# Large tiles moved to multiples of 2048 bytes, and the first block's probabilities transposed on TensorE

## What is computed

```python
x = x + tanh(g_xattn) * attention(layernorm(x), ctx, ctx)   # causal, softmax, concat @ Wo.T + bo
x = x + tanh(g_ffn) * ffn(layernorm(x))
# ffn: h = silu((x @ w1.T) * s1) * ((x @ w2.T) * s2)         256 -> 1024
#      h = gelu((h @ h1.T) * hs1); h = gelu((h @ h2.T) * hs2) 1024 -> 1024, twice
#      return (h @ w3.T) * s3                                1024 -> 256
```

## Time and profile before

| | |
|---|---|
| median of three runs | 1804.46 us (1802.91 to 1806.54) |
| the profiled execution | 1806.88 us, of which the span from the first to the last instruction is 1804.8 us |
| TensorE busy | 1730.7 us, 96% |
| VectorE, ScalarE, GpSimd busy | 1321.6, 1306.7, 1106.8 us |
| mean granted TensorE clock | 0.985 of full |
| first FFN matmul | 89.43 us after the start |
| span per block after it | 1715.4 us over 31 blocks of FFN beside attention and one alone |

### The profile page before, as it was taken

One profiled execution on the slowest core, in us unless ns is written; L12 is line 12 of the kernel. 1 busy time (PEld: TensorE's weight loads), 2 busy tenths in 40 slices (PEclk: granted clock), 3 DMA queues, 4 the chain that ended last, 5 costly groups with the idle time before them and its releaser, 6 DMA issues.

```text
span 1804.8 us, 39555 instructions
## 1 busy us (share of the span) xinstructions
PE 1730.7 (96%) x11014; PEld 1465.8 (81%) x11014; DVE 1321.6 (73%) x2803; ACT 1306.7 (72%) x3014; POOL 1106.8 (61%) x1646
## 2 busy tenths in 40 slices
PE   3399999999999999999999999999999999999998
PEld 2288888888888888888888888888888888888876
DVE  5767777777777777777777777777778777777764
ACT  3477777777777777777778777778777777777764
POOL 4666566567556567656567656656655656755652
PEclk8699999999999999999999999999999999999999
DMA  9944545544455544445554454554445554445420
GB/s 288 242 108 109 131 128 142 141 111 116 122 134 134 139 121 113 120 128 134 139 129 114 114 131 128 145 136 113 114 129 132 137 139 114 114 121 134 117 59 7
DMA packets 370970, 231.37 MB, mean 128 GB/s; under 512 B 283136, under 2 KB 340736, under 8 KB 369408
## 3 DMA queue, kind: packets, MB, share of 16 engines
q1 hardware_dynamic: 368784, 219.23, 47.7%
q10 hardware_dynamic: 2160, 11.81, 1.9%
HBM read 113.53 MB, written 41.94 MB: 86 GB/s over the span
## 4 chain that ended last, share of the span: by engine, by line
PE 91%; issue 2%; DMA 2%; POOL 2%; ACT 1%; DVE 1%; SPq 1%; POOLq 0%; DVEq 0%; ACTq 0%
PE ffn L976 71%; PE work L916 12%; PE s_bank L951 3%; PE pv L967 3%; PE work L1056 2%; DMA pT<-p_parts 1%; POOL p_parts L468 1%; POOL p_parts L466 1%; DMA aw<-in_attn_w 0%; DMA q<-q_saved 0%; POOL hb L513 0%; ACT probs L821 0%; SPq L360 0%; SPq L356 0%; POOL ha L508 0%
## 5 line engine op out<-in xcount | busy, mean ns | idle before, releaser
L976 PE MATMUL ffn<-hb,W 128*128 128x512 f32 x2048 | 512.2, 402 | 1.4 <-POOL hb L513 1.4
L976 PE MATMUL ffn<-ha,W 128*128 128x512 f32 x2048 | 492.1, 397 | 0.8 <-POOL ha L508 0.8
L658 DVE TENSOR_REDUCE full<-ffn 128x256 f32<-128x512 f32 x512 | 349.5, 688 | 194.1 <-PE ffn L976 194.1
L976 PEld LDWEIGHTS ffn<-ha,W 128*128 128x128 f32 x2048 | 379.4, 188 | 90.6 <-POOL ha L508 1.7
L976 PEld LDWEIGHTS ffn<-hb,W 128*128 128x128 f32 x2048 | 377.6, 188 | 86.3 <-POOL hb L513 2.3
L821 ACT ACTIVATE probs<-probs,exp_bias 128x128 f32<-128x128 f32 x1024 | 320.4, 390 | 50.8 <-POOL exp_bias L476 49.7
L468 POOL TENSOR_TENSOR p_parts<-probs,p_parts 128x512 f16<-128x512 f32 x256 | 300.4, 1173 | 20.5
L513 POOL TENSOR_TENSOR hb<-full,hb 128x256 fp32r<-128x256 f32 x256 | 187.3, 737 | 122.3 <-ACT full L839 116.5
L976 PE MATMUL ffn<-x2T_hi,W 128*128 128x256 f32 x1024 | 258.5, 287 | 1.4 <-DVE x2T_lo L754 0.9
L839 ACT ACTIVATE full<-full,cols 128x256 f32<-128x256 f32 x512 | 253.1, 494 | 0.0
L976 PE MATMUL ffn<-x2T_lo,W 128*128 128x256 f32 x1024 | 252.9, 284 | 0.0
(11 more groups left out here) (82 smaller groups left out, 2341.1 us busy)
## 6 DMA issues: line engine op xcount, KB each, us to landing
k<-k_saved SPq DMA_DIRECT2D x256, 128.0 KB, 2.8
q<-q_saved SPq DMA_DIRECT2D x256, 128.0 KB, 2.8
k_saved<-k_parts SPq DMA_DIRECT2D x32, 512.0 KB, 3.2
q_saved<-q_parts SPq DMA_DIRECT2D x32, 512.0 KB, 3.1
wnat<-in_ffn_w ACTq DMA_DIRECT2D x11, 1024.0 KB, 7.5
xT<-in_x_T SPq DMA_DIRECT2D x32, 256.0 KB, 3.3
cT<-in_ctx_T SPq DMA_DIRECT2D x32, 256.0 KB, 3.4
x_in<-in_x SPq DMA_DIRECT2D x32, 256.0 KB, 3.7
```

Source lines behind the costliest of these rows:

```text
L658: dve.tensor_reduce(full[:, m % 4], src[:].rearrange("p (a t) -> p t a", a=2), AX_X, ALU.add).then_inc(done, 1)
L976: return pe.matmul(dst, w, h, **flags)
```

## The change

1. The small tiles are declared first, then a tile of 264 floats that nothing reads or writes (`to_boundary`), then W, aw and all large tiles. With the scratch region cut from 8192 to 4096 bytes, W starts at 14336, a multiple of 2048 bytes, and so does every tile behind it whose predecessors are whole multiples of 2048 bytes, which all large tiles are.
2. In block 0 the eight D steps go. In their place TensorE transposes the 8 x 128 columns of p_parts into a bank of the FFN (step T, 16-bit), and ScalarE copies the bank to pT (step R). R stands in for the landing of the transfer: it raises pT_in by 16. T.k waits for the split, and for R.(k-2), whose bank it overwrites; R.k waits for T.k and PV.(k-2).
3. PROLOGUE is a new order of the same steps, with T and R for D. ORDER is unchanged; the blocks from 1 on keep their DMA transposes.
4. GpSimd makes a 16-bit copy of the identity matrix before it clears k4, and VectorE and TensorE wait for one more of GpSimd's constants before they start.

```diff
 PROLOGUE = steps("""
-    q.0 kw Q.0 K qw q.1 k st W.0 kr.0 v Q.1 V W.1 S.0 S.1 e.0 S.2 W.2 s.0 m.0 S.3 Q.0+ qr.0 K+ s.1 i.0 m.1 s.2 e.1
-    S.4 kr.1 m.2 i.1 S.5 s.3 lx+ m.3 i.2 lr W.3 lc+ q.0+ W.4 s.4 m.4 p.0 e.2 S.6 S.7 s.5 e.3 W.5 p.1 s.6 lt+ qr.1
-    i.3 D.0 D.1 m.5 Q.1+ D.2 p.2 nh.0 i.4 k+ PV.0 PV.1 PV.2 p.3 i.5 nm.0 D.3 e.4 qw+ W.6 p.4 PV.3 p.5 PV.4 i.6 kw+
-    s.7 st+ W.7 PV.5 To.0 O.0 e.5 D.4 q.1+ m.6 V+ m.7 S.0+ W.8 nm.1 i.7 D.5 PV.6 W.9 p.6 nh.1 W.10 p.7 F.0 rx PV.7
-    S.1+ qr.0+ To.1 O.1 e.6 nm.2 nh.2 e.7 o.0 s.0+ kr.0+ n2.0 F.1 D.6 nm.3 nh.3 to.0 v+ to.1 m.0+ X2.0 i.0+ s.1+ o.1
-    n2.1 e.0+ D.7 kr.1+ x2.0 rx+ qr.1+ lr+ x2.1 m.1+ X2.1
+    Q.0 k q.0 q.1 W.0 st i.0 W.1 v K Q.1 e.0 i.1 V W.2 S.0 kw qw e.1 S.1 W.3 kr.0 i.2 S.2 S.3 Q.0+ s.0 m.0 p.0 qr.0
+    lr p.1 s.1 m.1 R.0 T.0 rx s.2 K+ m.2 W.4 s.3 p.2 q.0+ S.4 W.5 i.3 i.4 e.2 W.6 PV.0 R.1 T.1 s.4 m.3 S.5 qr.1 m.4
+    p.3 s.5 lc+ i.5 W.7 kr.1 m.5 s.6 i.6 Q.1+ p.4 PV.1 p.5 S.6 i.7 nm.0 m.6 nh.0 T.2 nm.1 S.7 T.3 lt+ p.6 s.7 PV.2
+    e.3 R.2 lx+ PV.3 T.4 k+ qw+ T.5 PV.4 qr.0+ p.7 PV.5 T.6 e.4 e.5 R.3 m.7 To.0 q.1+ nh.1 O.0 e.6 st+ R.4 W.8 R.5
+    nh.2 V+ W.9 W.10 to.0 PV.6 T.7 F.0 e.7 o.0 S.0+ PV.7 To.1 R.6 F.1 nh.3 kw+ R.7 nm.2 s.0+ kr.0+ n2.0 O.1 nm.3
+    X2.0 X2.1 v+ m.0+ to.1 i.0+ o.1 x2.0 kr.1+ n2.1 rx+ S.1+ lr+ x2.1 s.1+ e.0+ qr.1+ m.1+
 """)
...
-        W = sb("W", [P, W_COLS], F32R)
-        aw = sb("aw", [P, 4, KE, E])
-        wq, wk, wv, woT = (aw[:, i] for i in range(4))
+        COPIES = 4
+        PSLOTS = 4
+        TSLOTS = 2
+
...
+        ident16 = sb("ident16", [P, P], F16)
...
+        wait_holder = sb("wait_holder", [P, 1])
+
+        to_boundary = sb("to_boundary", [P, TO_BOUNDARY])
+
+        W = sb("W", [P, W_COLS], F32R)
+        aw = sb("aw", [P, 4, KE, E])
+        wq, wk, wv, woT = (aw[:, i] for i in range(4))
+        x_in = sb("x_in", [P, ROWS, E])
         xres = sb("xres", [P, ROWS, E])
...
+        pT_turned = sem("pT_turned")
...
-                    if kind == "D" and here:
+                    if kind == "D" and here and not (isinstance(blk, int) and blk == 0):
...
+            pool.wait_ge(pool_const, 6)
+            pool.tensor_copy(ident16[:], ident[:]).then_inc(pool_const, 1)
             pool.memset(k4[:].bitcast(F32), 0.0).then_inc(keys_cleared, 1)
...
-                    pool.wait_ge(pool_const, 9)
+                    pool.wait_ge(pool_const, 10)
...
+                    if kind == "R" and weights:
+                        act.wait_ge(pT_turned, k + 1)
+                        wait(act, pv_ready, k + 1 - TSLOTS)
+                        act.activation(pT[:, k % TSLOTS].rearrange("p a h s -> p (a h s)"),
+                                       ffn[1 + k % 2][:].bitcast(F16), ACT.Copy).then_inc(pT_in[k % 2], 16)
...
+                        if kind == "T" and weights:
+                            pe.wait_ge(p_hi_ready, k + 1)
+                            pe.wait_ge(p_lo_ready, k + 1)
+                            pe.wait_ge(wq_centred, 1)
+                            if k > 1:
+                                pe.wait_ge(pT_in[k % 2], 16 * (k // 2))
+                            turned = ffn[1 + k % 2][:].bitcast(F16)
+                            for i in range(8):
+                                last = pe.transpose(turned[:, i * P:(i + 1) * P], p_parts[:, k % 2, i // 4, i % 4],
+                                                    ident16[:])
+                            last.then_inc(pT_turned, 1)
...
-    nc = bacc.Bacc("TRN2", target_bir_lowering=False, num_devices=1, dynamic_dma_scratch_size=8192)
+    nc = bacc.Bacc("TRN2", target_bir_lowering=False, num_devices=1, dynamic_dma_scratch_size=4096)
```

More of the change, by code:

```diff
@@ L23 @@
 LOW_BITS = 0xFFF
+TO_BOUNDARY = 264
 MASKED = -1e9
@@ L121, in program @@
         flag = sb("flag", [1, 1], I32)
-        x_in = sb("x_in", [P, ROWS, E])
         stats = sb("stats", [P, ROWS, 6])
@@ L128, in program @@
         rstd = sb("rstd", [P, ROWS])
+        vs = sb("vs", [P, ROWS, H, VCOLS], BF16)
+        negmax = sb("negmax", [P, PSLOTS, 4])
+        exp_bias = sb("exp_bias", [P, PSLOTS, 4])
+        head_sum = sb("head_sum", [P, 2, PAIR, D])
+        rden = sb("rden", [P, ROWS, H])
+        stats2 = sb("stats2", [P, ROWS, 6])
+        moments2 = sb("moments2", [P, ROWS, 2])
+        var_eps2 = sb("var_eps2", [P, ROWS])
+        rstd2 = sb("rstd2", [P, ROWS])
+        wait_holder = sb("wait_holder", [P, 1])
[4 more added lines that the diff above has]
+        x_in = sb("x_in", [P, ROWS, E])
         xres = sb("xres", [P, ROWS, E])
@@ L131, in program @@
         cT = sb("cT", [P, KE, TOK])
-        COPIES = 4
         q_parts = sb("q_parts", [P, 2, ROWS, KE, P], F32R)
@@ L139, in program @@
         k_saved = nc.dram_tensor("k_saved", [2, ROWS, P, KE * P], F32, kind="Internal").ap()
-        vs = sb("vs", [P, ROWS, H, VCOLS], BF16)
         v_rest = sb("v_rest", [P, ROWS, E])
-        PSLOTS = 4
         probs = sb("probs", [P, PSLOTS, 4, P])
-        negmax = sb("negmax", [P, PSLOTS, 4])
-        exp_bias = sb("exp_bias", [P, PSLOTS, 4])
         p_parts = sb("p_parts", [P, 2, 2, 4, P], F16)
-        TSLOTS = 2
         pT = sb("pT", [P, TSLOTS, 2, 4, P], F16)
-        head_sum = sb("head_sum", [P, 2, PAIR, D])
-        rden = sb("rden", [P, ROWS, H])
         heads = sb("heads", [P, ROWS, E])
@@ L154, in program @@
         x1_prev = sb("x1_prev", [P, ROWS, E])
[L155 to L158, removed]
         x2n = sb("x2n", [P, ROWS, E])
-        wait_holder = sb("wait_holder", [P, 1])
         x2T_hi = sb("x2T_hi", [P, KE, TOK], F32R)
@@ L548, in _ @@
         def _(dve):
-            dve.wait_ge(pool_const, 9)
+            dve.wait_ge(pool_const, 10)
             def scale_constants():
@@ L1079, in _ @@
             any_inexact = []
-            pe.wait_ge(pool_const, 9)
+            pe.wait_ge(pool_const, 10)
             run(False, 0)
```

## The result

The changed kernel takes 1782.03 us, the median of four runs (1781.86 to 1783.53), where the kernel before took 1805.5 us beside it (1802.91 to 1808.18): ratio 0.9871, 95% interval 0.9855 to 0.9886. The forecast was 1800.5 us, in a range from 1793 to 1806.5. The sign was right. The size was wrong by a factor of six: 23.5 us came where 3.9 were forecast.

A forecast was written before the change was run, and what follows sets the result against it. TensorE, busy 96% of the span, bounds the kernel; only prologue length and matmul pace can move it. Start and middle 1.5 us plus tail 2.4 make 3.9 us off the 1804.46 us median: 1800.5 us, range 1793 to 1806.5.

The forecast's parts named there:

- Aligned tiles: Large tiles moved to multiples of 2048 bytes: priced at nothing for the matmuls, with the extreme outcomes left to two rivals.
- rival 3: All blocks: tile starts set the matmul pace; 125 us less, 1676 us, or a part of it; chance 0.11.
- Rival 4: All blocks: aligned tiles slow matmuls as two operands on one boundary; 0.002 us each, 15 us, 1816 us; chance 0.03.
- The prologue: Stretch before the first FFN matmul: 3.9 us shorter, that matmul at about 85.5 us instead of 89.4.
- T: Block 0, eight TensorE transposes per step: 0.9 us, lower end 0.39, upper end twice 0.86; covered except for the last.
- R: Block 0, ScalarE copy of 1024 elements out of PSUM: 1.1 us, between 0.6 and 1.89; eight make 8.8 us.
- First scores: Start of the prologue: K's copy first, Q's parts about 1.3 us earlier, scores at 30.8 us instead of 31.98.
- The middle: ScalarE's queue from first to eighth exponentials: 36.35 us of work, 3.0 of waits, ending 72.75 instead of 74.25 us.
- The tail: From the end of the eighth exponentials to the first FFN matmul, 15.2 us before: 2.4 us less.
- Rival 1: Prologue hardly shorter: ScalarE keeps its old 6.3 us of chunk waits; 0.6 us left, about 1804; chance 0.18.
- Rival 2: Prologue slower: R in ScalarE's queue holds the chunk chain, from R of 1.7 us on; about 1807; chance 0.08.
- The clock: TensorE's half speed in the first FFN matmuls: 1.7 us either way; gained only if transposes count as activity.

The follow-up runs named there:

- the fourteen profiles: Profiled kernels that all have the new prologue and differ only in where their tiles lie: first FFN matmul between 81.9 and 85.9 us, 84.0 on average.
- e11: Changed kernel with the old tiles and DMA transposes instead of T and R, two block 1 loads moved ahead: 1832.97 us, ratio 1.0149.
- e2: Changed kernel with the tiles where they were before (new order, T and R kept): 1800.74 us, ratio 0.9965.
- e10: Kernel before, old order and old tiles, with T and R in place of the DMA transposes in block 0: 1819.94 us, ratio 1.0071.
- e3: Changed kernel with all large tiles moved together by 32 bytes: 1784.12 us, ratio 0.9875.
- e4: Changed kernel with all large tiles moved together by 128 bytes: 1784.10 us, ratio 0.9875.
- e1: Kernel before with only the new places of the tiles; old order and DMA transposes stay: 1796.78 us, ratio 0.993.
- e16: The changed kernel itself, run again on the same chip as e15: 1782.60 us, ratio 0.9856.
- e9: Changed kernel with three gaps: x2T 64 bytes past a multiple of 2048, ha 256 past, hb 1024 past: 1778.26 us, ratio 0.984.
- e12: Changed kernel with k4 and every tile behind it moved by 64 bytes, except ha and hb: 1781.18 us, ratio 0.9852.
- e15: Changed kernel with x2T (and full and y behind it) moved by 64 bytes, ha back at its multiple: 1777.69 us, ratio 0.9827.
- e5: Changed kernel with a 32-byte gap ahead of ha and hb, W staying at its multiple of 2048: ratio 0.9951.
- e6: Changed kernel with a 64-byte gap ahead of ha and hb, W staying at its multiple of 2048: ratio 0.989.
- e8: Changed kernel with a 608-byte gap ahead of ha and hb, restoring the old distance from W to ha: ratio 0.997.
- e7: Changed kernel with a 128-byte gap ahead of ha and hb, W staying at its multiple of 2048: ratio 0.9956.
- e14: Changed kernel with x2T_hi 128 bytes past a multiple of 2048, x2T_lo 192, ha 192, hb 224: 1793.95 us, ratio 0.992.
- e13: Changed kernel with W and aw moved to 96 bytes past a multiple of 2048, other tiles at multiples: 1801.14 us, ratio 0.9963.

## Why the prediction was wrong

**Aligned tiles: the step that failed.** The prediction's sum has no term for the pace of the matmuls; 16.8 us came from it. The prediction priced aligned tiles at nothing because "W starts at a multiple of 128 bytes, x2T 32 bytes past a multiple of 64, and both have the same pace". The comparison was of the wrong thing. It set the start of one moving tile against that of another, while what counts is how far the moving tile lies from the stationary one, modulo 256 bytes. Every FFN matmul of the kernel before had the same distance but for its sign: W 128 past, x2T, ha and hb 224 past, 96 between them. So the trace held one distance only, and "both have the same pace" was no evidence for any price. It is the range, more than the value, that this should have changed: with one setting of a variable in the trace, nothing bounds its effect. The range left rival 3 out whole, though it had a chance of 0.11. (By the prediction's own sum its low end is 1793.8, not 1793.)

**Rival 3** had the mechanism in part, with a chance of 0.11. Its test ("0.225 us or less") did not come true: 0.2276 and 0.2296. Its premise, that the places make the whole difference between half of the half-clock distance and the full-clock one, is wrong in size. Of the 0.020 us that it wanted back for 512 columns, 0.006 and 0.004 came, and of the 0.012 for 256 columns, none: three of the four kinds got 0.0014 to 0.0023 us slower, and only those that read x2T_lo got 0.0014 faster. **Rival 4**, aligned tiles slow the matmuls as two operands on the same boundary, priced 0.002 us, is right for 256 columns and wrong for 512. Both rivals had held that one rule goes for all matmuls; their net is 17.7 us.

**The prologue: 3.9 us forecast, 6.8 measured in this execution.** The transfers went out of TensorE's way, as forecast. But 3.9 lies within the 3.5 to 7.6 of the fourteen profiles, so the total alone says little about its terms. By the terms:
- *T* was forecast at 0.9 us, the chain has 0.87 for eight. *R* was forecast at 1.1 us; tile pT's view has eight of 1.0 us, and the next instruction starts 0.92 us after an R does:

```profile
L872 ACT ACTIVATE pT<-ffn x8: 999/1011/1024, 41.3 to 73.5; 128x1024 f16<-128x1024 f16 x8
```

- *First scores* were forecast at 30.8 us and came at 31.45 in TensorE's timeline. K's copy is earlier, as forecast, but the second half of Q is not: 19.02 us in ScalarE's timeline, where the prediction had it behind K's at once. The parts of Q, written from 19.95 us on, are what the scores wait for. TensorE's row first, then ScalarE's.

```profile
31.45 0.80 PE L959 MATMUL s_bank<-k,q 128*128 128x256 f32 x2 [10.74 <-DMA q<-q_saved]
```

```profile
16.14 0.60 ACT L816 ACTIVATE k_parts<-work 128x512 fp32r<-128x512 f32 x1 [10.00 <-PE work L924]
19.02 0.39 ACT L808 ACTIVATE q_parts<-work 128x256 fp32r<-128x256 f32 x1 [2.00 <-PE work L924]
...
68.24 1.26 ACT L824 ACTIVATE probs<-probs,exp_bias 128x128 f32<-128x128 f32 x4
69.41 1.00 ACT L872 ACTIVATE pT<-ffn 128x1024 f16<-128x1024 f16 x1
73.45 1.02 ACT L872 ACTIVATE pT<-ffn 128x1024 f16<-128x1024 f16 x1 [3.03 <-issue]
```

- *The middle* is the term that was mis-sized. The eighth exponentials end at 69.5 us (68.24 + 1.26), forecast 72.75. ScalarE's first exponentials start at 34.07, so the same list of work took 35.4 us where the sum had 36.35 and 3.0 of waits, 3.9 more. Of the 35.4 us ScalarE is busy 33.0 and idle 2.5 (us, ScalarE busy with instructions, clock, DMA share, GB/s):

```profile
34.07:69.50 35.43, 32.96 (x52) 0.60 0.79 279
```

  The sum charged seven issues of chunk loads with 2.4 us of ScalarE's time. They take next to none of it, because they run while an instruction of ScalarE's is still at work. Four exponentials with an issue among them take 1.17 us to the start of the next instruction, as four without one do (from 52.05 to 53.22 us):

```profile
37.05 0.39 ACT L824 ACTIVATE probs<-probs,exp_bias 128x128 f32<-128x128 f32 x1
37.18 0.33 ACTq L786 DMA_DIRECT2D wnat<-in_ffn_w  x1
37.34 0.97 ACT L824 ACTIVATE probs<-probs,exp_bias 128x128 f32<-128x128 f32 x3
38.22 1.90 ACT L802 ACTIVATE W<-wnat 128x2048 fp32r<-128x2048 f32 x1
```

  Six R at 0.92 and not 1.1 make another 1.1 us, and the waits 0.5. The roundings wait 1.0 us in all:

```profile
L802 ACT ACTIVATE W<-wnat 128x2048 fp32r<-128x2048 f32 x9 | 17.1, 1904 | 1.0 <-DMA wnat<-in_ffn_w 0.9
```

  Before it was 6.3 us, for tests and chunks; I had kept 3.0, on the ground that their causes stay. The transfers were one of the causes: the DMA share is 0.68 from 58 to 70 us instead of 1.04, and the roundings wait 12.9 us for chunks in e11, which has the transfers, where they wait 0.6 us in e2, which has the same order but for two loads, the same tiles, and T and R.
- *The tail*, forecast at 12.8 us from the eighth exponentials to the first FFN matmul (15.2 - 2.4), took 13.1. The last R stands 3.0 us for T and the split, which was in the sum.

**Rival 1** (ScalarE goes on waiting for chunks) fell by that row. **Rival 2** (R holds the chunk chain) did not happen in the changed kernel, where all of ScalarE's waits at R are 4.2 us; but e10 shows that the mechanism is real and worth 12 us where R stands at a bad place. The prediction had its condition (4 us of waits more) and was right to keep it.

**The clock.** The prediction let it add 1.7 us either way. It cost 1.2. In the changed kernel TensorE's first FFN matmuls with 256 columns follow each other at 0.213 us, the lower level (1.2 GHz), until 88.3 us, then at 0.120, the upper (2.4 GHz):

```profile
83.42 0.41 PE L984 MATMUL ffn<-x2T_lo,W 128*128 128x256 f32 x1
83.63 0.41 PE L984 MATMUL ffn<-x2T_hi,W 128*128 128x256 f32 x1
...
90.42 0.28 PE L984 MATMUL ffn<-x2T_hi,W 128*128 128x256 f32 x1
90.54 0.28 PE L984 MATMUL ffn<-x2T_lo,W 128*128 128x256 f32 x1
```

The granted clock by stretch (us, busy PE, PEld, DVE, ACT, POOL, clock, DMA share, GB/s), of the kernel before first and of the changed kernel second, shows how long that lasted:

```profile
90.00:93.40 3.40, 3.40 (x18) 3.40 (x17) 1.56 (x3) 0.63 (x2) 2.06 (x4) 0.50 0.29 104
```

```profile
82.60:88.40 5.80, 5.79 (x27) 5.79 (x28) 3.77 (x7) 2.68 (x9) 2.48 (x4) 0.50 0.66 196
```

Before, the first FFN matmuls still ran at the upper level, from 89.4 to 90.0 us, and the lower lasted 3.4 us; now it lasts 5.8 us, and the 2.4 us more do the work of 1.2. With the T steps TensorE was busy 6.2 of the 12 us from 58 to 70, where it was 1.0, and the granted clock there was 0.50 in both. From 71.4 to 78.1 us it was 1.00, and from 78.3 to the first FFN matmul, where TensorE was busy 1.6 of 4.3 us, 0.50 again.

The Trainium skill, "TensorE: Matmul & The Clock Gate", section "Part 4: PE-mode transpose", says that transposes don't count as activity for the clock; by this rule the T steps bring nothing. The trace doesn't speak against it, since nothing was gained, but other matmuls stand between the T steps, and no run here shows the rule by itself.

The Trainium skill, "DMA: Bandwidth & Descriptors", section "How a descriptor splits into AXI transactions", says that a piece which doesn't start at a 256-byte boundary begins with a transaction from the boundary below it, and that the bytes before its start are fetched unused. The profiles agree: the writes of q_parts and k_parts land after 3.1 and 3.2 us at the median in the kernel before and in e2, e3 and e4, whose parts start 224, 32 or 128 bytes past a boundary, and after 2.9 in the changed kernel and in e1, where they start at one. A row of e3's page, then two of the changed kernel's:

```profile
k_saved<-k_parts SPq DMA_DIRECT2D x32, 512.0 KB, 3.2
```

```profile
k_saved<-k_parts SPq DMA_DIRECT2D x32, 512.0 KB, 2.9
q_saved<-q_parts SPq DMA_DIRECT2D x32, 512.0 KB, 2.9
```

It moved no time that can be seen: e3 and e4 have the rest of the changed kernel.

## What to carry to other kernels

Where TensorE is busy 96% of the span, look at its pace per matmul before its waits: here the pace gave 16.8 us and the prologue 6.8. Where the stationary tile lies against the moving one is a part of the pace: try gaps of 0 and 64 bytes between them, apart for each moving width, before the schedule is worked on. A variable that has one setting in the trace has no price in it; give it a range, not a zero. Moving transposes from the queues to TensorE paid here only together with an order in which no copy of theirs held the engine that issues the loads.

## What the runs showed of the hardware

Float32r matmuls of 128x128, at the full clock and back to back, by the distance from the start of the stationary tile to that of the moving one, modulo 256 bytes:

| distance | 512 columns | 256 columns | from |
|---|---|---|---|
| 0 | 0.2275 to 0.2281 (ha), 0.2291 to 0.2302 (hb) | 0.1192 to 0.1204 | after, e1, e3, e4, e16; what reads ha or hb in e9, e12 and e15 |
| 32 | 0.2332, 0.2330 | 0.1177 | e5 |
| 64 | 0.2304, 0.2302 | 0.1164 to 0.1171 | e6, e9, e15 |
| 96 | 0.2332 to 0.2340 | 0.1176 to 0.1212 | before, e2, e8, e10, e11 |
| 128 | 0.2324, 0.2330 | 0.1184 to 0.1194 | e7, e14 |
| 160 | 0.2340, 0.2340 | 0.1175, 0.1182; W moving 0.1198 | e13 |
| 192 | 0.2331 | 0.1163 to 0.1168 | e14 |
| 224 | 0.2331 | not seen | e14 |

The 256-column values at 32, 96 (e8) and 128 (e7) are those with W moving over ha, for which the distance is taken from W to ha as well; e12, with x2T at 64, has 0.1180 and 0.1178 and stands outside. The float32 projections (work<-aw,cT, 256 columns) kept 0.216 us, the median of their distances, in every run. Two things are open. Why the sign turns with the width: no run has another width than these two. And why the scores, whose own two tiles k4 and q4 are at distance 0 before and after, went from 0.1182 to 0.1198 us. It is not their own distance alone: in e13 and e14 k4 and q4 are at distance 0 too, and the scores take 0.1186 and 0.1183 us, though W and aw alone, or x2T, ha and hb with the two tiles between them, were moved. So the tiles of the matmuls around them have a part in it; a matmul's distance to its successor may take in the load of the successor's weights, from another tile, but none of the runs tells that apart. So the table holds for runs of matmuls that take their weights from one tile; at a change of tiles none of its numbers is shown.
